# GRU step loop with attention ahead of it: one PSUM transpose per gate instead of one for two, and the convolutions on GpSimd taken eight steps at a time

## The reference

```python
x = x + attention(x)                    # 16 heads, modulated RMS norm, q/k norm, o + o @ W_out
x = x + gru(cond, x)                    # 512 steps in sequence, initial state cond
#   r = sigmoid(i_r + h_r); z = sigmoid(i_z + h_z); n = tanh(i_n + r * h_n)
#   h = (1 - z) * n + z * h,  h_* = h @ W_hh + b_hh
x = x + causal_conv(x, taps = cond)     # depthwise, 4 taps: tap k of feature d is cond[k, d]
x = x + causal_conv(x, taps = cond) + b # the same taps, and a bias
```

## Time and profile before

| | |
|---|---|
| median of 3 runs | 2158.68 us (2157.4 to 2159.33) |
| the profiled execution's own time | 2154.03 us |
| its span in the trace | 2152.2 us |
| granted TensorE clock, mean | 0.997 of full speed |
| TensorE busy | 2087.6 us, 97% |
| VectorE busy | 1386.3 us, 64% |
| ScalarE busy | 1174.6 us, 55% |
| GpSimd busy | 1122.1 us, 52% |
| first transpose of a GRU step | at 594.1 us |

### The profile page before, as it was taken

One profiled execution on the slowest core, in us unless ns is written; L12 is line 12 of the kernel. 1 busy time (PEld: TensorE's weight loads), 2 busy tenths in 40 slices (PEclk: granted clock), 3 DMA queues, 4 the chain that ended last, 5 costly groups with the idle time before them and its releaser, 6 DMA issues.

```text
span 2152.2 us, 183070 instructions
## 1 busy us (share of the span) xinstructions
PE 2087.6 (97%) x76192; PEld 1574.0 (73%) x76192; DVE 1386.3 (64%) x5140; ACT 1174.6 (55%) x5995; POOL 1122.1 (52%) x3876
## 2 busy tenths in 40 slices
PE   8999999999999999999999999999999999999998
PEld 2222222222389999999999999999999999998887
DVE  4344444344367777777777777777777777777776
ACT  3444444443255555555555555555555555555555
POOL 0243323323146666666666666666666666666665
PEclk9999999999999999999999999999999999999999
DMA  6000000001122212221222221222121212210001
GB/s 255 1 1 1 1 1 1 1 21 60 38 68 52 54 48 54 52 54 51 69 56 54 52 53 49 55 59 65 49 57 48 58 47 60 65 30 10 5 7 19
DMA packets 218062, 95.89 MB, mean 45 GB/s; under 512 B 170216, under 2 KB 213480, under 8 KB 217320
## 3 DMA queue, kind: packets, MB, share of 16 engines
q1 hardware_dynamic: 217032, 92.00, 16.4%
q10 hardware_dynamic: 928, 2.65, 0.3%
HBM read 26.30 MB, written 12.58 MB: 18 GB/s over the span
## 4 chain that ended last, share of the span: by engine, by line
PE 63%; DVE 8%; issue 1%; DMA 0%; SPq 0%; ACT 0%; DVEq 0%
PE ps L1199 57%; DVE arena L1024 5%; PE ps L1227 4%; PE ps L1238 2%; DVE arena L1030 1%; DVE arena L1036 1%; DVE arena L1041 1%; DMA arena<-arena 0%; DVE arena L1108 0%; DVE arena L1111 0%; SPq L952 0%; DVE arena L1114 0%; ACT ps L1132 0%; DVE arena L1117 0%; DVE seq L1054 0%
## 5 line engine op out<-in xcount | busy, mean ns | idle before, releaser
L1199 PE MATMUL ps<-whh,arena 128*4 128x128 f32 (+1 forms) x65536 | 1447.7, 246 | 36.4 <-DVE arena L1041 33.0
L1199 PEld LDWEIGHTS ps<-whh,arena 128*4 128x4 f32 x65536 | 1299.9, 87 | 142.4 <-DVE arena L1041 64.4
L1024 DVE STREAM_TRANSPOSE arena<-ps 128x128 f32<-128x128 f32 x1024 | 436.3, 426 | 226.3 <-PE ps L1199 226.2
L1157 ACT ACTIVATE arena<-arena 128x8 f32<-128x8 f32 x1024 | 215.9, 211 | 637.1 <-DVE arena L1024 637.0
L1271 POOL TENSOR_TENSOR arena<-tap,seq 128x32 f32<-128x32 f32 x1020 | 230.6, 258 | 217.7 <-DVE seq L1054 217.7
L437 DVE TENSOR_REDUCE top<-ps 128x2 f32<-128x1024 f32 x128 | 150.8, 1220 | 253.7 <-PE ps L693 253.6
L1041 DVE TENSOR_TENSOR_SCAN arena<-arena 128x24 f32<-128x24 f32 x1024 | 213.7, 209 | 145.1 <-ACT arena L1168 145.1
L1132 ACT ACTIVATE ps<-arena 128x128 f32<-128x128 f32 x1026 | 269.6, 263 | 0.4 <-PEq L207 0.4
L1271 POOL TENSOR_TENSOR arena<-tap,arena 128x32 f32<-128x32 f32 x1020 | 231.0, 257 | 66.5 <-POOL arena L1281 66.5
L1030 DVE STREAM_TRANSPOSE arena<-ps 128x64 f32<-128x64 f32 x1024 | 257.8, 252 | 12.1 <-PE ps L1199 1.7
L268 POOL TENSOR_TENSOR arena<-arena 128x2048 f32<-128x2048 f32 x16 | 72.8, 4548 | 344.3 <-ACT arena L343 344.3
(11 more groups left out here) (96 smaller groups left out, 1385.2 us busy)
## 6 DMA issues: line engine op xcount, KB each, us to landing
arena<-arena SPq DMA_DIRECT2D x216, 114.0 KB, 2.2
arena<-arena SPq DMA_DIRECT2D x112, 128.0 KB
arena<-seq SPq DMA_DIRECT2D x224, 55.0 KB
arena<-gi_d SPq DMA_DIRECT2D x248, 32.0 KB
gi_d<-arena SPq DMA_DIRECT2D x96, 57.0 KB, 2.3
out<-seq SPq DMA_DIRECT2D x14, 256.0 KB
seq<-in_x SPq DMA_DIRECT2D x3, 1024.0 KB, 15.2
whh<-in_w_hh SPq DMA_DIRECT2D x1, 3072.0 KB, 22.5
```

The lines of the kernel that those rows point to most:

```text
L1024: e.transpose(trn[:, h].rearrange("p q (i c s) -> p q c i s", c=2, s=2)[:, :, :, :, 0], bank[RN[h]][:, 0:P].rearrange("p (q c i) -> p q c ...
L1157: e.activation(r_d0[:, h].rearrange("p (i s) -> p i s", s=2)[:, :, 1], trn[:, h, 0, 0:2 * NH].rearrange("p (i s) -> p i s", s=2)[:, :, 0], ...
L1199: last = e.matmul(bank[dst[h]][32 * G:32 * G + B, 0:n], hv, wv[:, k, gates, G, 64 * h:64 * h + 64], start=False, stop=k2 == 1 and k == C - ...
```

## The change

Three things. `turn_rn(h)` becomes two transposes of 64 columns, r first and n behind it, each counting up `s_tr` (which now goes up by 6 a step, not 4). The sigmoid of r waits for the first only; `seed_rn(h)`, which overwrites the bank, and `scan_n(h)` wait for the second. On GpSimd the convolutions go in blocks of `NB = 8` steps: 13 instructions for eight steps, on 128 elements (16 items x 8 steps; the tap is broadcast along time and the tap of the current step has 1 added, which takes in the residual) or 256 (`conv_halves`). `let_in(m)` waits for one more GRU step before a group of them, so that the instructions are spread over the eight steps that follow the block. The last eight columns, no longer two, are VectorE's after the last step.

```diff
-        tap = sb("tap", [P, TAPS, NI, 2])
-        b3x = sb("b3x", [P, NI, 2])
+        tap = sb("tap", [P, TAPS, NI])
+        b3x = sb("b3x", [P, NI])
...
-        POOL_OPS, END_OPS = 9, 5 + 2 * TAPS
+        NB, POOL_OPS, END_OPS = 8, 7, 13
+        wide = NB * NI
+        def conv_part(i):
+            return prd[:, wide * i:wide * i + wide].rearrange("p (i s) -> p i s", s=NB)
+        def along(v):
+            return v.rearrange("p (i s) -> p i s", s=1).broadcast_to([P, NI, NB])
+        def conv_product(e, src, k, t):
+            return e.tensor_tensor(conv_part(k), along(tap[:, k]), src[:, :, bass.ds(t + k, NB)], ALU.mult)
+        def conv_halves(e):
+            return e.tensor_tensor(prd[:, 4 * wide:6 * wide], prd[:, 0:2 * wide], prd[:, 2 * wide:4 * wide], ALU.add)
...
                     def turn_rn(h):
                         e.wait_ge(st["s_rn"], half[h])
-                        e.transpose(trn[:, h].rearrange("p q (i c s) -> p q c i s", c=2, s=2)[:, :, :, :, 0],
-                                    bank[RN[h]][:, 0:P].rearrange("p (q c i) -> p q c i", q=2, c=2)
-                                    ).then_inc(st["s_tr"], 1)
+                        for q in range(2):
+                            e.transpose(trn[:, h, q].rearrange("p (i c s) -> p c i s", c=2, s=2)[:, :, :, 0],
+                                        bank[RN[h]][:, 64 * q:64 * q + 64].rearrange("p (c i) -> p c i", c=2)
+                                        ).then_inc(st["s_tr"], 1)
...
                     def scan_n(h):
+                        e.wait_ge(st["s_tr"], n_at[h])
                         e.wait_ge(st["s_sig"], half[h])
...
-                            e.wait_ge(st["s_tr"], turned[2 * h])
+                            e.wait_ge(st["s_tr"], turned[3 * h])
...
-                            e.wait_ge(st["s_tr"], turned[2 * h + 1])
+                            e.wait_ge(st["s_tr"], turned[3 * h + 2])
...
                         reset(0)
+                        e.wait_ge(st["s_tr"], turned[1])
                         seed_rn(0, s)
                         update(0)
                         new(0)
                         reset(1)
+                        e.wait_ge(st["s_tr"], turned[4])
                         seed_rn(1, s)
...
-                with e.Fori(0, T // 2 - 1) as it:
+                with e.Fori(0, T // NB - 1) as it:
+                    t = e.snap(it * NB)
+                    def let_in(m):
+                        wait(st["s_x3"], it * NB + NB + m)
+                    let_in(0)
+                    conv_product(e, seq, 0, t)
+                    conv_product(e, seq, 1, t)
+                    let_in(1)
+                    conv_product(e, seq, 2, t)
+                    conv_product(e, seq, 3, t).then_inc(s, 1)
+                    let_in(2)
+                    wait(s, it * POOL_OPS + 1)
+                    conv_halves(e).then_inc(s, 1)
+                    let_in(3)
+                    wait(s, it * POOL_OPS + 2)
+                    e.tensor_tensor(seq2[:, :, bass.ds(it * NB + PAD, NB)], conv_part(4), conv_part(5), ALU.add).then_inc(s, 1)
+                    wait(s, it * POOL_OPS + 3)
+                    conv_product(e, seq2, 0, t)
+                    let_in(4)
+                    conv_product(e, seq2, 1, t)
+                    conv_product(e, seq2, 2, t)
+                    let_in(5)
+                    conv_product(e, seq2, 3, t).then_inc(s, 1)
+                    let_in(6)
+                    wait(s, it * POOL_OPS + 4)
+                    conv_halves(e).then_inc(s, 1)
+                    let_in(7)
+                    wait(s, it * POOL_OPS + 5)
+                    e.tensor_tensor(conv_part(6), conv_part(4), conv_part(5), ALU.add).then_inc(s, 1)
+                    wait(s, it * POOL_OPS + 6)
+                    e.tensor_tensor(seq[:, :, bass.ds(t, NB)], conv_part(6), along(b3x[:]), ALU.add).then_inc(s, 1)
+                    wait(s, it * POOL_OPS + 7)
```

More of the change, by code:

```diff
@@ L522, in _ @@
                     e.tensor_tensor(d, d, ident[:], ALU.add).then_inc(d_wout, 1)
[L523 to L527, removed]
+                for c in range(C):
+                    items = slice(B * c, B * c + B)
+                    e.tensor_copy(tap[:, 0:PAD, items], vecT[:, c, 0:PAD].rearrange("p (k a) -> p k a", a=1).broadcast_to([P, PAD, B]))
+                    e.tensor_scalar(tap[:, PAD, items], vecT[:, c, PAD:TAPS].broadcast_to([P, B]), 1.0, None, ALU.add)
+                    e.tensor_copy(b3x[:, items], vecT[:, c, R_B3:R_B3 + 1].broadcast_to([P, B]))
                 for n in range(NS):
@@ L935, in store @@
             if first + n < T:
-                e.wait_ge(st["s_pool"], POOL_OPS * ((first + n) // 2))
+                e.wait_ge(st["s_pool"], POOL_OPS * ((first + n) // NB))
             else:
@@ L1019, in step @@
                     h4 = count(2 * t + 4)
+                    n_at = (count(6 * t + 2), count(6 * t + 5))
                     now = count(t + PAD)
@@ L1097, in _ @@
                         step(it * 2 + v, v)
[L1100 to L1103, removed]
+                t, done = T - NB, s_end
+                e.wait_ge(st["s_pool"], POOL_OPS * (T // NB - 1))
                 e.wait_ge(st["s_x3"], T)
[L1105 to L1121, removed]
+                for k in range(TAPS):
+                    conv_product(e, seq, k, t).then_inc(done, 1)
+                e.wait_ge(done, 4)
+                conv_halves(e).then_inc(done, 1)
+                e.wait_ge(done, 5)
+                e.tensor_tensor(seq2[:, :, t + PAD:T + PAD], conv_part(4), conv_part(5), ALU.add).then_inc(done, 1)
+                e.wait_ge(done, 6)
+                for k in range(TAPS):
+                    conv_product(e, seq2, k, t).then_inc(done, 1)
+                e.wait_ge(done, 10)
+                conv_halves(e).then_inc(done, 1)
+                e.wait_ge(done, 11)
+                e.tensor_tensor(conv_part(6), conv_part(4), conv_part(5), ALU.add).then_inc(done, 1)
+                e.wait_ge(done, 12)
+                e.tensor_tensor(seq[:, :, t:T], conv_part(6), along(b3x[:]), ALU.add).then_inc(done, 1)
             @block.scalar
@@ L1151, in _ @@
                         half = (e.snap(2 * t + 1), e.snap(2 * t + 2))
-                        turned = [e.snap(4 * t + i) for i in (1, 2, 3, 4)]
+                        turned = [e.snap(6 * t + i) for i in range(1, 7)]
                         following = e.snap(t + 1)
                         def reset(h):
-                            e.wait_ge(st["s_tr"], turned[2 * h])
+                            e.wait_ge(st["s_tr"], turned[3 * h])
                             e.activation(r_d0[:, h].rearrange("p (i s) -> p i s", s=2)[:, :, 1],
```

25 lines of the change are left out of this document (1 added, 24 removed).

## The result

| | median of the runs | ratio to before | 95% interval |
|---|---|---|---|
| before | 2158.68 us | | |
| after | 2165.05 us | 1.0031 | 1.0024 to 1.0038 |

The profiled execution of after took 2161.26 us, with a span of 2159.3, where before had 2154.03 and 2152.2. Three readings of the two traces divide the 7.0 us between the unrounded spans: the first transpose of the GRU comes at 594.4 and not 594.1 (+0.3); from there to the start of the last add to `seq` it is 1557.2 and not 1551.6 (+5.5 unrounded); from there to the end of the span 7.7 and not 6.5 (+1.2).

What follows compares the result with a forecast made beforehand. The loop from one GRU step to the next was taken as the bound, through scan_h(0) in 176 bare steps, with TensorE full in the other 336. -1.8 + 0.6 + 1.2 = 0.0 us gave 2158.7, range 2148 to 2174.

Steps and rivals of the forecast that it cites:

- GpSimd's longer instructions hold scans that count: Rival on GpSimd: slower strided products hold scan_n(0) 0.3 and make scan_h(0) end 0.13 later; 13 us, 2172; chance 0.13.
- scans of 0.3 or more: Sign in the trace after: if scans this long (us) appear, the forecast is wrong.
- GpSimd's term in Part 2: GpSimd's blocks: scan_n(0) held 0.08 to 0.18, hidden in the stretch of parts, costing in the last 64 steps; +0.6 us.
- let_in(7): GpSimd group with two dependent instructions, forecast like let_in(3) to end at 0.88 to 0.98 and hold scan_n(0) 0.08 to 0.18.
- 2 in 8: In the rival on GpSimd's longer instructions: two steps of every eight pay, x 512 x 0.10 = 13 us.
- The law of the hold: VectorE instruction with two SBUF inputs, started inside a GpSimd instruction, is held for the time left less 0.19.
- Part 1: Two transposes for one on VectorE: queue order leaves scan_h(0) 0.01 earlier in 176 bare steps; -1.8 us.
- The rival of transposes in series: Rival on VectorE: second transpose waits for the first's end, loop grows 0.11 in bare steps; 46 us, 2205; chance 0.12.
- Part 3: The end on VectorE: eight products of 128 elements for eight of 32, and longer adds; +1.2 us.

Runs made afterwards that it cites:

- extra_covered: product_moved with an unused 256-element GpSimd add behind the first product of let_in(4), in a step with a part on TensorE; 2165.47 us, ratio to before 1.0043.
- no_let_in: After without the waits let_in(1) to let_in(7), so all 13 GpSimd instructions follow each other from step 0 of a block; 2234.37 us, ratio to before 1.0354.
- no_pool_one: After with one transpose for r and n, and GpSimd's convolutions of the GRU stage left out; 2158.88 us, ratio to before 1.0003.
- no_pool: After with GpSimd's convolutions of the GRU stage left out, the two transposes kept; 2158.09 us, ratio to before 0.9999.
- product_moved: After with the second convolution's first product moved from behind let_in(3) to let_in(4), its third to behind let_in(5); 2155.59 us, ratio to before 0.9992.
- split_only: Before with only the two transposes for one, GpSimd still working two steps at a time; 2159.57 us, ratio to before 1.0008.
- The loop of eight steps: product_moved with TensorE's loop turned by one step and its last loop eight steps long, not two; 2292.89 us, ratio to before 1.0625.

## Why the prediction was right or wrong, step by step

I forecast no change (2158.7) and got +6.4 us: inside the wide range of 2148 to 2174, outside the forecast's own of 2154 to 2163. That the wide range held is no merit of the sum, in which the term that decided was nearly nothing. The rival "GpSimd's longer instructions hold scans that count" came true, with a chance of 0.13 and a price of 13 us against 7.7 in the stage. My own sign of being wrong, scans of 0.3 or more, appeared.

- **The step that failed** is GpSimd's term in Part 2: `scan_n(0)` is held 0.08 to 0.18 and "in the stretch of parts that is hidden; in the last 64 steps it costs 0.08 in 16 of them". The product ends at 0.98, as forecast, and the size of a hold was nearly right (measured 0.19). Its place was wrong both ways. `let_in(3)` opens in step k = 3, and 3 mod 4 is the bare step, v = 3, each time: my own text gives both numbers and I did not put them together. So the hold fell where nothing covers it, once in eight steps, at (1339.3 - 1331.7) / 55 = 0.14 each in steps 16 to 456. In the last 64, where I charged it, VectorE's add to `seq` and with it GpSimd come 0.26 later in the step's time, and the scan is past. The term was +0.6; it is +7.6 in steps 16 to 456 and none in the last steps. extra_covered adds that even a covered step would have paid: a part covers 0.06.
- **`let_in(7)`**, which I priced like `let_in(3)`, lengthens `scan_n(0)` by only 0.02, from 0.19 to 0.21, and the step k = 7 takes 2999 ns. Its second instruction runs from 0.41 to 0.82, so only 0.17 of it is left when the scan starts; that of `let_in(3)` runs from 0.57 to 0.98. That is why the rival's "2 in 8" came out as one.
- **The law of the hold** taken from the earlier trace rows, the time left less 0.19, was nearly right. Step 203 of after: 0.32 of the product is left when the scan starts, which lasts 0.19 longer. extra_covered: 0.32 left, 0.17 longer. no_let_in: 0.65 left, 0.50 longer, and 0.39 left, 0.24 longer. It is the time left less 0.13 to 0.15 for scans, and the profile's ends on GpSimd are rough. The Trainium skill ("SBUF — State Buffer", section "Who interferes with whom") has the second to start blocked until the first finishes; the traces agree but for these 0.15.
- **Part 1**: the second transpose costs what I took. Two of 64 columns take 0.43 to 0.44 together where one of 128 took 0.43, `scan_h(0)` starts 0.30 behind the r transpose of half 1 and takes 0.17, and half 1's first transpose stays at 0.88. The rival of transposes in series is refuted by this. The Trainium skill's sentence that I took for it ("VectorE: DVE Perf Modes", "The DRAIN you can't avoid") again does not hold here; the same section adds that a next instruction that is not held starts earlier, which I left out, and which the traces bear out: the n transpose starts 0.17 behind an r transpose that lasts 0.31. Not foreseen: that 0.31, where a transpose alone has 0.25, so the sigmoid starts at 0.34 and not 0.28. The gain on the chain was mis-sized: `scan_h(0)` ends 0.033 earlier (1.354 for 1.386) and not 0.01, since it starts 0.30 and not 0.32 to 0.34 behind r. That the split, put at 1.8 us, measured 1.5 (no_pool_one against no_pool) is therefore partly luck. Its place differs: the gain is 2.3 us in the last 55 steps, where a step is 0.04 shorter, and in steps 16 to 456 product_moved is 0.6 us slower than before, though its bare steps are 0.01 shorter.
- **Nine single steps** more than make the 0.6. Steps 24, 52, 126, 172, 255, 273, 338, 375 and 430 of product_moved are 0.1 to 0.3 longer than others of their place, 2.1 us together; after and no_pool have the same nine among theirs, split_only has eleven others (2.5 us), while before has one of 0.08 and no_pool_one none up to step 448. So they come with the split, and without them product_moved would be 1.5 us ahead of before in steps 16 to 456. In them VectorE stands still with its data there, as between `turn_z(1)` and `scan_n(1)` of step 24 in product_moved:

```profile
673.61 0.25 DVE L1051 STREAM_TRANSPOSE arena<-ps 128x64 f32<-128x64 f32 x1
...
674.18 0.19 DVE L1058 TENSOR_TENSOR_SCAN arena<-arena 128x16 f32<-128x16 f32 x1 [0.32 <-DVE arena L1051]
```

  Each of the nine begins 1.6 to 2.9 us ahead of a packet of instruction queue q14, of which the kernels with the split have 68 and those with one transpose 54. That VectorE's unrolled program, longer by two transposes a step, stands still for its code is thus likely, but no run tests it.
- **Part 3**: +1.2 us forecast, +1.2 measured.

Sum as measured: -0.4 in steps 0 to 16, +7.6 for the holds, +0.6 and -2.3 for the rest of the steps, +1.2 at the end: +6.7. With the 0.3 of a later start that is the 7.0 between the spans.

product_moved is the best version: 9.5 us under after, 7.7 of them in the stage, and with a ratio of 0.9992 (0.9983 to 1.0001) not to be told from before. The small gain is in its stage (-2.2 us unrounded, one profiled execution of each) only.

## What to carry to other kernels

When a helper's instructions are spread over the steps of a loop, write the helper's period and the main loop's period side by side, and mark the steps in which nothing covers the chain. A covered step saved here only 0.06 of a hold, so look above all at where an instruction falls within the step: 0.26 us decided between a hold of 0.19 and none. A total of waits that stays equal, with another count and another longest, can be two opposite changes.

## What the hardware showed that I had not expected

- A scan held by a long GpSimd instruction mostly does not start late in the records, it lasts longer: 0.36 to 0.40 and up to 0.69, where 0.19 is usual. (In split_only one started 0.11 late.) No wait names GpSimd for it: look at durations.
- The end of TensorE's loop costs 0.27 us where TensorE is full and 0.025 where it would wait for the state (2998 ns with it, 2973 without).
- The loop of eight steps fetched its code again (2.10 MB of instructions for 0.79). Most of its steps took 3.0 to 4.3 us, and one at the end of each pass but the last 11.3 to 12.0: 4.6 on average.
- The spread between kernels of equal GRU stage comes from ahead of it. The first transpose comes between 594.1 and 598.8 us, and later in a kernel with a lower granted clock ahead of it: by 594.4 in the six traces with the clock at half (1.2 GHz) for 7 to 10 us in all before it, at 596.6 to 598.8 in the six with 14 to 21. The same window of before (granted clock 0.99) and of no_pool (0.97; its first transpose comes at 598.8):

```profile
100.00:300.00 200.00, 194.42 (x1752) 53.49 (x1748) 85.89 (x92) 95.45 (x131) 74.80 (x21) 0.99 0.01 1
```

```profile
100.00:300.00 200.00, 194.60 (x1732) 53.36 (x1728) 84.75 (x90) 93.87 (x129) 72.11 (x20) 0.97 0.00 1
```

All kernels run the same program up to there, but for the setup of the taps. Terms of 2 us in the GRU stage can be read from that stage and are lost in the total.
